# Third layer of the bias network in bursts of eight pairs instead of four, with longer rings of tiles

## What is computed

```python
pos  = grid_q[:, :, None, :] - grid_kv[:, None, :, :]
bias = jnp.sign(pos) * jnp.log1p(jnp.abs(pos))
bias = jax.nn.relu(bias @ cpb_w1 + cpb_b1)
bias = jax.nn.relu(bias @ cpb_w2 + cpb_b2)
bias = (bias @ cpb_w3 + cpb_b3).reshape(b, GROUPS, H * W, Hd * Wd)
sim  = jnp.einsum('bhid,bhjd->bhij', qh, kh) + bias
```

## Time and profile before

| | |
|---|---|
| median of three runs | 1319.81 us |
| the profiled execution's own time | 1319.84 us |
| its span in the trace | 1317.2 us |
| PE busy | 1258.5 us, 96% |
| ACT busy | 810.7 us, 62% |
| DVE busy | 780.3 us, 59% |
| POOL busy | 685.8 us, 52% |
| the loop, first `offset` to last `layer3` | 69.54 to 820.78 us of the span |

### The profile page before, as it was taken

How to read it: one execution, slowest core, us unless ns; L and a number is a source line. 1 busy time by engine, 2 the same in 40 slices (tenths; PEclk the granted TensorE clock), 3 DMA queues, 4 the chain that set the end, 5 groups by cost and what they waited for, 6 DMA issues and landing times.

```text
span 1317.2 us, 25029 instructions
## 1 busy us (share of the span) xinstructions
PE 1258.5 (96%) x10420; PEld 500.5 (38%) x10420; DVE 780.3 (59%) x1002; ACT 810.7 (62%) x976; POOL 685.8 (52%) x387
## 2 busy tenths in 40 slices
PE   6399999999999999999999999879999899999998
PEld 4332222222222222222222222644444555555554
DVE  6766666666666666666666664741001477777773
ACT  4677778777777777777777776333121255555553
POOL 3366666666666666666666664330000036666664
PEclk9599999999999999999999999989999999999999
DMA  2340110111011011011101100000001712232212
GB/s 74 95 139 2 33 33 1 34 34 33 2 33 34 1 34 33 12 23 34 34 1 33 34 1 2 0 0 0 0 1 66 261 26 58 57 77 62 61 34 76
DMA packets 22504, 51.63 MB, mean 39 GB/s; under 512 B 5622, under 2 KB 10870, under 8 KB 22264
## 3 DMA queue, kind: packets, MB, share of 16 engines
q1 hardware_dynamic: 20084, 43.74, 12.1%
q10 hardware_dynamic: 2308, 6.30, 1.8%
HBM read 36.64 MB, written 11.15 MB: 36 GB/s over the span
## 4 chain that ended last, share of the span: by engine, by line
PE 91%; DVE 4%; ACT 2%; DMA 1%; issue 1%; ACTq 0%; POOL 0%; POOLq 0%; SPq 0%; DVEq 0%
PE ps L940 33%; PE ps L949 18%; PE ps L1110 6%; PE ps L931 5%; PE ps L1140 5%; PE ps L1151 5%; PE ps L1047 4%; PE ps L1057 4%; PE ps L1161 2%; PE ps L1076 2%; PE ps L1086 1%; PE ps L1034 1%; PE ps L1202 1%; DVE big L673 1%; PE ps L1000 1%
## 5 line engine op out<-in xcount | busy, mean ns | idle before, releaser
L940 PE MATMUL ps<-big,w 64*64 64x512 f32 x4096 | 484.1, 589 | 0.0
L534 ACT ACTIVATE big<-ps 128x1024 f32<-128x1024 f32 x256 | 261.9, 1023 | 178.9 <-PE ps L940 178.9
L732 DVE TENSOR_SCALAR big<-big 128x1024 f32<-128x1024 f32 x256 | 177.7, 694 | 263.9 <-POOL big L435 263.9
L435 POOL TENSOR_TENSOR big<-qpad 128x1024 f32<-128x1024 f32 x128 | 244.5, 1910 | 146.8 <-PE ps L940 71.0
L726 DVE TENSOR_TENSOR big<-qpad,ps 128x1024 f32<-128x1024 f32 x256 | 310.9, 1214 | 7.8 <-ACT ps L513 5.4
L435 POOL TENSOR_TENSOR big<-qpad,V 128x1024 f32<-128x1024 f32 x128 | 244.5, 1910 | 129.4 <-PE ps L940 72.3
L534 ACT ACTIVATE big<-ps,vec 128x1024 f32<-128x1024 f32 x256 | 283.8, 1109 | 0.0
L949 PE MATMUL ps<-big,w3s 128*32 128x512 f32 x2048 | 246.2, 598 | 1.3 <-ACT big L534 1.3
L940 PEld LDWEIGHTS ps<-big,w 64*64 64x64 f32 x4096 | 146.5, 133 | 207.0 <-issue 112.7
L460 POOL TENSOR_TENSOR big<-big 128x1024 f32<-128x1024 f32 x32 | 76.4, 2389 | 228.8 <-ACT big L623 188.8
L802 DVE TENSOR_REDUCE amax<-ps 128x1 f32<-128x1024 f32 x128 | 154.6, 1210 | 44.5 <-PE ps L1110 43.1
(11 more groups left out here) (156 smaller groups left out, 1086.1 us busy)
## 6 DMA issues: line engine op xcount, KB each, us to landing
raw<-s_f SPq DMA_DIRECT2D x32, 512.0 KB, 5.9
h1l<-k_d SPq DMA_DIRECT2D x33, 128.0 KB, 3.6
h1h<-q_d ACTq DMA_DIRECT2D x33, 128.0 KB, 4.2
X<-in_x SPq DMA_DIRECT2D x2, 1024.0 KB, 6.3
q_d<-XN SPq DMA_DIRECT2D x4, 512.0 KB, 3.5
k_d<-XN SPq DMA_DIRECT2D x4, 512.0 KB, 4.0
q_d<-big SPq DMA_DIRECT2D x4, 512.0 KB, 3.9
k_d<-big SPq DMA_DIRECT2D x4, 512.0 KB, 5.3
```

Of the source, the lines that this page charges most:

```text
L435: pool.tensor_tensor(h1[m % HRING].rearrange("p (y a b) -> p y a b", y=2, b=W), u.unsqueeze(2).to_broadcast(shape), a[:, :, HALF // W * hf ...
L534: act.activation(h2[m % H2RING], z2[m % ZRING], ACT.Relu, bias=v("cb2") if m % 2 else 0.0).then_inc(h2_ready, 1)
L732: dve.tensor_scalar(h1[m % HRING], h1[m % HRING], 0.0, None, ALU.max).then_inc(h1_ready, 1)
L940: last = pe.matmul(z2[m % ZRING][CH * y:CH * (y + 1), HALF * x:HALF * (x + 1)], w2[CH * x:CH * (x + 1), :], h1[m % HRING][CH * x:CH * (x + ...
```

## The change

BURST goes from 4 to 8, HRING from 4 to 6, H2RING from 8 to 12. The two further `h1` tiles and the four further `h2` tiles lie in a new name `ring` on the memory of `h1h`, `h1l` and `qk3`: the code allocates `ring`, gives it back, and allocates those three on the same place. The other small tiles (`amax`, `mparts`, `ones`, `smax` and their like) are allocated earlier. ACT's wait for a free `h2` tile is rewritten for the new ring. AHEAD1 goes from 6 to 8. Both parts of the preparation, `first_sums` and `first_bounds`, now stand together behind `relu2` of the tenth pair of a piece.

```diff
--- before.py
+++ after.py
@@ -29,8 +29,8 @@
 
 CHUNKS, PAIRS = 8, 32
 PIECE = 16
-AHEADQ, AHEAD1 = 2, 6
-HRING, H2RING, BURST, ZRING = 4, 8, 4, 3
+AHEADQ, AHEAD1 = 2, 8
+HRING, H2RING, BURST, ZRING = 6, 12, 8, 3
 PARTS_S = [0, 0, 1, 1, 0, 2]
 PARTS_W = [0, 1, 0, 1, 2, 0]
 NR = len(PARTS_S)
@@ -130,10 +130,18 @@
         hx = m2[:, 0:4, :].rearrange("p a b -> p (a b)")
         sel = m2[0:2, 4:7, :].rearrange("p a b -> p (a b)").rearrange("p (a k n) -> p a k n", a=3, k=4)
 
+        amax = [sb(f"amax{i}", [P, NK]) for i in range(HEADS3)]
+        mparts = sb("mparts", [NK, 2, P], fp32r)
+        ones = sb("ones", [P, D])
+        smax, ssum, srec = ([sb(f"{n}{i}", [P, NK]) for i in range(2)] for n in ("smax", "ssum", "srec"))
+
+
+        with nc.sbuf_tensor("ring", [P, 6, N], fp32) as ring:
+            pass
         h1h, h1l = sb("h1h", [P, 4, HALF], fp32r), sb("h1l", [P, 4, HALF], fp32r)
-        h1 = [big[:, 4 + i, :] for i in range(HRING)]
-        h2 = [big[:, i + i // 4 * 4, :] for i in range(H2RING)]
-        smax, ssum, srec = ([sb(f"{n}{i}", [P, NK]) for i in range(2)] for n in ("smax", "ssum", "srec"))
+        qk3 = sb("qk3", [P, 2, N], fp32r)
+        h1 = [big[:, 4 + i, :] for i in range(4)] + [ring[:, 4 + i, :] for i in range(2)]
+        h2 = [big[:, i + i // 4 * 4, :] for i in range(8)] + [ring[:, i, :] for i in range(4)]
 
 
         pos, pp, pn, s3 = (BT[:, i, :] for i in range(4))
@@ -206,7 +214,6 @@
 
         V = big[:, 0:4, :].rearrange("p a b -> p (a b)").rearrange("p (n j d) -> p n j d", j=NK, n=G)
         rT = XN
-        qk3 = sb("qk3", [P, 2, N], fp32r)
         part = [[x[:, 2 * i + a, :].bitcast(fp32r) for a in range(2)] for x in (XN, big[:, 4:8, :]) for i in range(2)]
         QS = [h1h[:, 2 * i:2 * i + 2, :].rearrange("p a b -> p (a b)") for i in range(2)] + [qk3[:, 0, :]]
         KS = [h1l[:, 2 * i:2 * i + 2, :].rearrange("p a b -> p (a b)") for i in range(2)] + [qk3[:, 1, :]]
@@ -214,9 +221,6 @@
         PSUMS = [big[:, 11, :], BT[:, 14:16, :].rearrange("p a b -> p (a b)")]
         OT = [big[:, 10, QUARTER * i:QUARTER * (i + 1)] for i in range(2)]
         orec = [big[:, 10, QUARTER * i:QUARTER * (i + 1)] for i in (2, 3)]
-        amax = [sb(f"amax{i}", [P, NK]) for i in range(HEADS3)]
-        mparts = sb("mparts", [NK, 2, P], fp32r)
-        ones = sb("ones", [P, D])
 
         out_v = out.rearrange("b (c p) n -> p b c n", p=P)
         x_v = d["x"].rearrange("b (c p) n -> p b c n", p=P)
@@ -536,12 +540,11 @@
             for m in range(PAIRS * G):
                 act.wait_ge(z2_ready, m + 1)
                 if m >= H2RING:
-                    act.wait_ge(l3_done, m // BURST - 1)
+                    act.wait_ge(l3_done, (m - H2RING) // BURST + 1)
                 relu2(m)
                 if m // PIECE + 1 < 2 * G:
-                    if m % PIECE == 7:
+                    if m % PIECE == 9:
                         first_sums(m // PIECE + 1)
-                    if m % PIECE == PIECE - HRING:
                         first_bounds(m // PIECE + 1)
```

## The result

| | before | after |
|---|---|---|
| median | 1320.04 us (1318.76 to 1320.49, 4 runs) | 1303.08 us (1302.52 to 1305.59, 4 runs) |
| the profiled execution | 1319.84 us | 1303.46 us |
| its span | 1317.2 us | 1301.7 us |
| the loop, first `offset` to the first matmul behind it | 752.11 us (69.54 to 821.65) | 736.02 us (69.78 to 805.80) |

The ratio is 0.9877, with a 95% interval of 0.986 to 0.9894: faster by 1.2%. Forecast were 1304.3 us and a range of 1301 to 1310.5.

What follows compares the result with a forecast made beforehand. PE's own instruction stream was taken to bound the loop, busy in all of 300 us. From 1319.84 us, 16.0 for 64 switches came off and 0.5 at the start was added: 1304.3 us, range 1301 to 1310.5.

Steps and rivals of the forecast that it cites:

- a switch of tile shape there and back costs 0.25 us: PE between layer 2 (64x64) and layer 3 (128x32): 0.10 going, 0.13 back, 0.02 in the first offset behind.
- 64 x 0.25 = 16.0 less 0.5 at the start: Whole loop: 64 switches there and back go, saving 16.0 us; 0.5 us is lost once at the start.
- the wait at the start: First round, behind the first burst: PE waits once, some 0.6 us, for relu2 of pair 10.
- the wait of 0.11 at the first burst: PE's wait of 0.11 us ahead of the first burst before the change, counted as going away.
- POOL and DVE keep up with a ring of six: POOL's sums and DVE's rectifiers: PE never waits for h1; POOL has 0.33 us to spare in 11.45.
- pair 17 at 7.86: POOL's sum of pair 17 with a ring of four: startable only behind pair 13, at 7.86 us, against 5.92.
- The preparation at the burst costs nothing: ACT's sums and bounds in each second burst: bounds run 3.9 to 4.6, before pair 10 at 5.02; no cost.
- rival 2: ACT's preparation comes too late: bound1 over 1.0 us later makes PE wait in 31 pieces; 6.2 us, 1310.5; chance 5%.
- before the run of layer 2 goes on: Expected sign in the later profile: ACT's L517, the bounds, ends before PE resumes layer 2 behind the burst.
- the spare 0.67 of ACT: ACT's relu2 of pair 10 ends at 6.04, PE wants its z2 for pair 13 at 6.71: 0.67 us spare.
- Rival 1: The 0.25 us belongs to the pairs, not the switch: only the start is lost, 1320.3 us; chance 4%.
- Rival 3: POOL becomes the bound: sums over 1.99 us set the round; at 2.39 the kernel takes 1406 us; chance 4%.

Runs made afterwards that it cites:

- the runs in 64x64 tiles: Changed kernel with layer 3 in layer 2's 64x64 tile shape, half its products left out: 1287.09 us with bursts of eight, 1286.58 with bursts of four.
- the ring of five: Changed kernel with an h1 ring of five tiles instead of six (HRING = 5), all else the same: 1337.63 us, 1.0133 of the kernel before.

## Why the prediction was right, step by step

- *PE's stream bounds the loop, and a switch of tile shape there and back costs 0.25 us of it.* Right. Four comparisons give it: 0.26 by the rounds of before and after, 0.26 by bursts of four with the new rings (1319.86 - 1303.08 = 16.78 for 64), 0.24 by bursts of two, 0.25 by doing without them. It was forecast from the difference of two equal runs of layer 2, 1.82 and 1.72, and from the ends of the burst; the runs in 64x64 tiles show that neither was a wait.
- *64 x 0.25 = 16.0 less 0.5 at the start.* The loop became 16.09 shorter. The price is 0.01 larger a switch, 0.6 us; the wait at the start was 0.36 and not 0.6, the wait of 0.11 at the first burst went, and 0.33 were lost to the clock. These nearly cancel; that the loop comes within 0.6 us of the 15.5 forecast is in part luck. Another 0.29 of the 16.38 lies outside the loop, where nothing was forecast.
- *POOL and DVE keep up with a ring of six.* Right to 0.1 us in each of POOL's four sums. That a ring of four would not do was said from one start (pair 17 at 7.86); the run shows the loss, 62 us with the preparation at its old places, and that it comes from pairs 23 and 25, one circle later than that sentence looked.
- *The preparation at the burst costs nothing.* Right in the steady loop. The run with the old places shows what the edit is worth, 11.0 us, and the ring of five what happens when the bounds start 1.8 us later (422.00 is 5.66 behind the end of layer 2 ahead of its burst, against 3.85): that is rival 2, at 0.87 us a piece (27 of the 35 us), and the wait of 0.73 puts the limit at 1.1, where 1.0 was forecast. One sign was put wrongly: L517 was to end "before the run of layer 2 goes on", but by the forecast's own times the bounds end at 4.6 and layer 2 goes on from 3.67. In the trace L517 ends 4.63 behind 401.45; what counts, that this is before `relu2` of pair 10 is due (5.01), held. And the spare 0.67 of ACT is that of pair 10, whose `z2` goes to an odd pair; for one whose `z2` goes to an even pair it is 0.45, as the run with the old places showed.
- *Rival 1*, that the price goes with the pairs, and with it the rule of "TensorE: Matmul & The Clock Gate" on loads pulled ahead (the Trainium skill, "Step-by-step: what each phase is for"): fell here. Loads are pulled ahead in the kernel with one shape, 0.42 us after the one before, and not across two shapes, 0.96. The rule holds inside a shape; the trace decides that it doesn't across.
- *Rival 3*, POOL's sums becoming longer: fell; all of its 256 sums took 1.907 to 1.917 us.

## What to carry to other kernels

When PE alternates between matmuls of different tile shapes, look at the same run of matmuls with and without a change of shape behind it, and the same for the way back (here 0.10 and 0.13 us, and 0.02 behind it); their sum, times the number of switches there and back that go, is what longer bursts of each shape can give. A longer burst has to be paid in ring tiles: work out, engine by engine, when each producer's next tile is due, and give the rings what the burst needs (here burst and two for the tiles it reads, six for those made meanwhile). Put side work of a rate-matched engine where PE does not need it: the same bounds of 0.70 us on ACT cost nothing beside a burst and 0.36 us a piece beside a run of layer 2.

## What the runs showed of the hardware that I had not expected

A change in the columns of a tile alone (64x64 to 64x32) costs PE as much as one in rows and columns: 1303.45 us against 1303.08. And a PE that has waited for another engine pays beyond the wait: 0.15 us from the end of DVE's rectifier to the matmul (rings of four and of five), 0.06 from the end of ACT's (423.72 to 423.78, ring of five), and 0.06 to 0.14 more in the layer 2 that starts from standstill (1.02 where 0.96 was due, 1.00 where 0.86 was).
